# Layer 0's single-precision matmuls, the turned rows and the gram product side by side; the sum over d and the halves of x1 one to four groups sooner

## What is computed

```python
x0 = xk = stack([tbl_f[ids[:, f]] for f in range(39)], axis=1)   # (512, 39, 16)
for W in (f0, f1, f2):                 # (39*39, 128), (128*39, 128), (128*39, 128)
    z = einsum('bfd,bgd->bfgd', x0, xk).reshape(b, f * g, d)
    xk = einsum('bpd,pm->bmd', z, W); outs.append(xk)
z = sum(concatenate(outs, axis=1), axis=-1)                       # (512, 384)
h = relu(concatenate([z, dense_ctx], 1) @ W_top1 + b_top1)
y = relu(h @ W_top2 + b_top2) @ W_top3
```

## Time and profile before

| | us |
|---|---|
| median of 3 runs | 699.26 (698.6 to 702.59) |
| the profiled execution | 700.51 |
| its span | 698.7 |
| PE busy | 643.2 (92%) |
| VectorE, ScalarE, GpSimd busy | 538.7, 518.5, 429.9 (77, 74, 62%) |
| layer 1's matmuls (L789, L790, L793) of 512 columns, groups for ScalarE | 175.3, 152.2, 152.4 |
| the products on ScalarE (L640), x1536 | 440.7 |
| the steps on VectorE (L532), x960 | 266.0 |
| the half-sums on VectorE (L503), x128 | 223.6 |

### The profile page before, as it was taken

How to read it: one execution, slowest core, us unless ns; L and a number is a source line. 1 busy time by engine, 2 the same in 40 slices (tenths; PEclk the granted TensorE clock), 3 DMA queues, 4 the chain that set the end, 5 groups by cost and what they waited for, 6 DMA issues and landing times. The chain is left out here.

```text
span 698.7 us, 11739 instructions
## 1 busy us (share of the span) xinstructions
PE 643.2 (92%) x2567; PEld 472.3 (68%) x2567; DVE 538.7 (77%) x1216; ACT 518.5 (74%) x1842; POOL 429.9 (62%) x416
## 2 busy tenths in 40 slices
PE   0578999999999999999999999999999999999988
PEld 0246777676767677777777676767676777776663
DVE  1426788888887979797988888888979797999880
ACT  1226688788797878787887888787878787888862
POOL 6876568686767676767678686767676534101330
PEclk9877999999999999999999999999999999999999
DMA  7551332231304040313131221313040320301000
GB/s 206 117 118 30 88 74 45 45 72 37 80 10 106 9 107 3 85 31 77 39 77 40 56 61 39 77 23 93 9 108 4 96 63 0 109 0 44 29 1 0
DMA packets 58221, 40.28 MB, mean 58 GB/s; under 512 B 36626, under 2 KB 41056, under 8 KB 58203
## 3 DMA queue, kind: packets, MB, share of 16 engines
q1 hardware_dynamic: 52376, 38.73, 22.1%
q0 software_dynamic: 5120, 1.29, 2.4%
q10 hardware_dynamic: 706, 0.06, 0.1%
HBM read 38.13 MB, written 1.94 MB: 57 GB/s over the span
## 5 line engine op out<-in xcount | busy, mean ns | idle before, releaser
L640 ACT ACTIVATE parts<-psa,x0c 128x128 f32<-128x128 f32 x1536 | 440.7, 431 | 94.6 <-PE psa L793 88.2
L532 DVE SCALAR_TENSOR_TENSOR parts<-psd,x0c,parts 128x128 f32<-128x128 f32 x960 | 266.0, 342 | 80.9 <-PE psd L793 64.1
L503 DVE TENSOR_REDUCE cur<-parts 128x64 f32<-128x1536 f32 x128 | 223.6, 1747 | 23.7 <-ACT parts L640 18.8
L789 PE MATMUL psa<-w1h,x1h 128*128 128x512 f32 x384 | 175.3, 457 | 5.9 <-issue 5.9
L793 PE MATMUL psa<-w1h,x1l 128*128 128x512 f32 x384 | 152.4, 397 | 0.0
L790 PE MATMUL psa<-w1l,x1h 128*128 128x512 f32 x384 | 152.2, 396 | 0.0
L359 POOL TENSOR_TENSOR z0l<-pairs,z0h 117x512 fp32r<-117x512 f32 x56 | 72.7, 1298 | 122.6 <-ACT z0h L596 122.4
L343 POOL DMA_INDIRECT emb<-tables,idx x130 | 126.7, 975 | 23.3 <-issue 19.8
L352 POOL TENSOR_TENSOR pairs<-x0t,pairs 117x512 f32<-117x512 f32 (+1 forms) x105 | 135.1, 1296 | 7.3 <-DMA x0t<-x_rows 6.6
L789 PE MATMUL psd<-w1h,x1h 128*128 128x512 f32 (+1 forms) x256 | 115.2, 450 | 12.1 <-DVE parts L532 12.1
L793 PE MATMUL psd<-w1h,x1l 128*128 128x512 f32 (+1 forms) x256 | 97.8, 382 | 0.0
(11 more groups left out here) (83 smaller groups left out, 524.5 us busy)
## 6 DMA issues: line engine op xcount, KB each, us to landing
pairs<-x_rows SPq DMA_DIRECT2D x113, 156.0 KB
pairs<-x_rows SPq DMA_DIRECT2D x30, 234.0 KB
x0t<-x_rows SPq DMA_DIRECT2D x16, 234.0 KB
emb<-tables,idx POOLq DMA_INDIRECT x130
x_rows<-emb SPq DMA_DIRECT2D x13, 72.0 KB
wt_sb<-w_top SPq DMA_DIRECT2D x1, 768.0 KB, 5.9
parts<-w SPq DMA_DIRECT2D x1, 704.0 KB, 4.9
x_rows<-emb SPq DMA_DIRECT2D x13, 40.0 KB
```

What stands on the lines that cost most here:

```text
L503: return dve.tensor_reduce(cur1[:, t % 2, first:end], terms[:, first:end, :, :], AX.XY, ALU.add)
L532: op = dve.scalar_tensor_tensor(acc, y[:, M * j:M * j + M], x0c[:, t, GF * g + j:GF * g + j + 1], acc, ALU.mult, ALU.add)
L640: op = act.activation(lanes(dst, j), y[:, M * j:M * j + M], ACT.Copy, scale=x0c[:, t, GF * g + j:GF * g + j + 1])
L789: pe.matmul(y[:, 0:n], hi, w1h[:, c], start=True, stop=False)
```

## The change

On PE, step k = 0 moves from behind group 5 of tile 0, and k = 1 from behind group 7, to behind group 9; the turn moves from group 8 to group 9 as well, so that k = 0, k = 1, the turn and the gram product follow one another. Steps 2, 3 and 4 each move one slot on, k = 5 stays, and k = 6 goes last, behind group 9 of tile 1 and in front of its gram product. The turn itself becomes four ordinary matmuls of 39 rows by 128 columns with a 39 x 39 identity, in place of four transposes of 117 rows with a 117 x 117 one. On VectorE the sum over d moves from the third group of tile 2 to its first, the low part of tile 0 from the fourth to the second, of tile 1 from tile 3's first to tile 2's third. On ScalarE the high part of tile 0 moves from the fifth to the second group of tile 2, of tile 1 from tile 3's first to tile 2's fourth, of tile 2 from tile 3's third to its first. In block 0 only steps 5 and 6 change places, and so they do in the prologue.

```diff
-L0_AT = {(0, 5): 0, (0, 7): 1, (0, 9): 2, (1, 1): 3, (1, 3): 4, (1, 5): 6, (1, 8): 5}
-L0_AT_FIRST = {(1, 6): 0, (1, 8): 1, (2, 0): 2, (2, 2): 3, (2, 4): 4, (2, 6): 6, (2, 8): 5}
-TURN_AT, TURN_AT_FIRST = (0, 8), (1, 5)
+L0_AT = {(0, 9): [0, 1], (1, 1): [2], (1, 3): [3], (1, 5): [4], (1, 8): [5], (1, 9): [6]}
+L0_AT_FIRST = {(1, 6): [0], (1, 8): [1], (2, 0): [2], (2, 2): [3], (2, 4): [4], (2, 6): [5], (2, 8): [6]}
+TURN_AT, TURN_AT_FIRST = (0, 9), (1, 5)
...
-L0_END = 5
+L0_END = 6
...
-SUM_AT, SUM_AT_FIRST = (2, 2), (3, 0)
-HIGH_AT = {(2, 4): 0, (3, 0): 1, (3, 2): 2}
+SUM_AT, SUM_AT_FIRST = (2, 0), (3, 0)
+HIGH_AT = {(2, 1): 0, (2, 3): 1, (3, 0): 2}
...
-LOW_AT = {(2, 3): 0, (3, 0): 1, (3, 1): 2}
+LOW_AT = {(2, 1): 0, (2, 2): 1, (3, 1): 2}
...
-        ident_sb = sb("ident_sb", [128, ROWS])
+        ident_sb = sb("ident_sb", [128, F])
...
-                act.activation(x0c[:, t, 0:F], pst[:, ROWS * t:ROWS * t + F], ACT.Copy).then_inc(x0c_ready, 1)
+                act.activation(x0c[:, t, 0:F], pst[:, F * t:F * t + F], ACT.Copy).then_inc(x0c_ready, 1)
...
-                    op = pe.transpose(pst[:, ROWS * t:ROWS * t + ROWS], x0t[0:ROWS, 128 * t:128 * t + 128], ident_sb[0:ROWS, :])
+                    op = pe.matmul(pst[:, F * t:F * t + F], x0t[0:F, 128 * t:128 * t + 128], ident_sb[0:F, :], start=True, stop=True)
...
-                            if (t, g) in l0_at:
-                                layer0(b + 1, l0_at[t, g])
+                            for k in l0_at.get((t, g), []):
+                                layer0(b + 1, k)
...
-            for k in [*(k for k in range(L0T) if k != L0_END), L0_END]:
+            for k in range(L0T):
                 layer0(0, k)
```

More of the change, by code:

```diff
@@ L660, in block_of @@
                                 scalars(b + 1, SCALARS_AT[t, n])
-            act.dma_start(ident_sb[0:ROWS, :], ident).then_inc(const_in, 16)
+            act.dma_start(ident_sb[0:F, :], ident).then_inc(const_in, 16)
             act.dma_start(mask_sb[:, :], mask).then_inc(const_in, 16)
@@ L918 @@
         "sample_mask": samples.astype(np.float32),
-        "identity": np.eye(ROWS, dtype=np.float32),
+        "identity": np.eye(F, dtype=np.float32),
     }
```

## The result

The kernel became slower: 723.1 us median (720.42 to 724.4, 4 runs) against 700.6 (698.6 to 702.59; with one run more than the 699.26 of the table ahead), ratio 1.032 with a 95% interval of 1.030 to 1.034. That is 22.5 us; 14.3 were forecast, and the range ended at 718.5.

What follows compares the result with a forecast made beforehand. TensorE, 92% busy, was taken to bound the kernel, with 2.04 us of stalls a block from VectorE's lateness. Order 7.7 plus turn 6.6 gave 14.3; 700.5 became 714.8, less 1.25 for the median: 713.5 us, range 702 to 718.5.

Steps and rivals of the forecast that it cites:

- stalls: PE's waits in a block: 1.42 + 0.19 + 0.60 + 0.42 = 2.63 us against 2.04, so +0.59.
- Part 2, the turn: On PE, eight passes with weight loads of 0.107, the first hidden: 0.86 us against 0.42, +0.44 a turn.
- The upper bound, 0.9: Most that PE's turn should take in us, from load plus handover: +0.48 a turn.
- Rival A: The turn on PE is cheap, lower bound 0.27 us by streaming alone; chance 0.20.
- Part 1, tile 2: ScalarE stands 1.91 us at x1h(0) for VectorE's sum; PE stalls 1.42 us, new, before group 8.
- Tiles 3 and 0: PE's stalls for VectorE: 0.19 us at tile 3 group 6, 0.60 at its group 9, 0.42 in tile 0.
- The wait at k = 0: PE's 0.71 us stall for x1l at layer 0's first step, in tile 0, would be gone.
- Rival D: Worse: 3.1 us on PE without a group behind group 9 starves VectorE, 0.4 more a block, 719; chance 0.07.
- rival C: Gains and losses cancel: x1l's 0.71 wholly won, turn cheap, stall 1.0, total 697 to 702; chance 0.05.
- Part 3, side by side: Four fewer borders a block between rounded and single precision on PE: taken as 0, upper bound 1 us.
- Part 4, the loads: Row loads and x0t's load issue some 2.4 us later, without a wait; cost 0.
- Rival B: Not slower: the sum reaches ScalarE in tile 2 in time, psa never runs full, 688; chance 0.10.

Runs made afterwards that it cites:

- Run 8: The changed kernel with the identity's buffer as wide as before, so that all buffers behind it lie where the kernel before has them; 725.6 us.
- run 3: The changed kernel with its turn made of ordinary matmuls of all 117 rows by a 117 x 39 identity; 719.5 us, ratio 1.027.
- run 2: The kernel before with the new turn of four 39-row matmuls alone, at its old place; 710.4 us, ratio 1.012.
- run 1: The changed kernel with the four transposes of 117 rows back in the turn, all else as changed; 712.6 us, 1.019 of before.
- run 4: The kernel before with layer 0's new order and the turn behind group 9; transposes, sum and halves as before; 706.5 us, ratio 1.008.
- run 6: The kernel before with the sum one VectorE group sooner, and high parts and two low parts later; 683.0 us, ratio 0.975.
- run 9: The kernel before, transposes kept, with the identity's buffer moved last and a gap of 39 columns in its place; 699.7 us, ratio 0.998.
- run 10: The kernel before with later halves, and the identity's buffer moved last with a gap in its place; 678.9 us, ratio 0.971.

## Why the prediction was wrong

The direction, the main stall and its place were right; the turn was priced too low, and the size was short by 8 us and the range with it. The budget of a block, in us:

| term | forecast | measured |
|---|---|---|
| turn | +0.44 | +0.79 |
| stalls | +0.59 | +1.26 |
| pace of the rounded matmuls | 0 | -0.46 |
| sum | +1.03 | +1.59 |

The pace is what remains of the period after the other two; 108 matmuls by 4.0 ns are 0.43 of it. Run 8, the changed kernel at the old placement, has the two forecast terms without the pace: +0.79 and +0.87 give its 38.97 to 0.01. So the forecast of the turn was short by 0.35 and that of the stalls by 0.28. That the unforeseen pace and the longer stalls that it brings (-0.46 and +0.39) nearly cancel is luck. As an estimate, the turn's 0.35 over its 15 times is 5.3 us and the stalls' 0.28 over 14 blocks 3.9; pace and its stalls give back 1.0, and the median of the kernel before came out 1.4 higher than in the forecast. Together they lead from 713.5 to 723.1. The turn's part alone leads to 718.8, just past the range; the stalls' alone would have stayed inside, at 717.4.

**Part 2, the turn, is the step that failed**: forecast 0.86, measured 1.21. Its loads are 0.11 apart, eight of them, as worked out; "one load at a time is ahead of the matmuls, so the first hides" is false where the matmuls go from 117 rows to 39 and from 39 to 128: there the load starts only 0.07 before the drawn end of the matmul before it (0.12 and 0.20). The upper bound, 0.9, was thus no bound; it is what run 3, all of whose loads but the first are exposed, takes (0.89). The bracket asked what a pass costs and not what its neighbours lose, though a row of the kernel before had the answer. Rival A, a cheap turn, which the range takes in, fell altogether: no run shows the 0.27 of its lower bound. A turn of 39 rows takes 1.21 in the changed kernel and in run 2, and the loads stand 108 to 112 ns apart with 39 rows and 110 to 112 with 117 (run 3).

**Part 1, tile 2**: the new stall is 1.71 for 1.42. ScalarE was let go 4.84 after the tile's first products began (340.70 to 345.54); forecast were 4.64. Two handovers were taken too short: products to VectorE's steps 0.12 (340.70 + 1.16 to 341.98), not 0.04, and the sum to ScalarE 0.18 (344.68 + 0.68 to 345.54), not 0.08. PE's faster pace brought it to the bank 0.1 sooner: runs 1 and 8, at the old pace, have 1.61 here.

**Tiles 3 and 0**: 0.41, 0.63 and 0.56 for 0.19, 0.60 and 0.42. At the old pace (run 1) they are 0.32, 0.60 and 0.41. So two of the three were right. Group 6 of tile 3 was 0.13 short at the old pace, which no run explains, and the rest goes with PE's faster pace. The wait at k = 0 went as said. Rival D, the starving of VectorE by the long stretch behind group 9, did not come: the stalls of run 4 are 0.43 and 0.79 in tile 3, and 0.47 and 0.79 in tile 0, where 0.4 and 0.8 were expected. The gain of rival C, 0.71 at k = 0, came, but the turn wasn't cheap and the stall was 1.71 for its 1.0.

**Part 3, side by side worth nothing**: right (run 4). **Part 4, the loads**: right as far as seen. In the block shown, PE waits for ScalarE and VectorE alone, and for no transfer and not for GpSimd.

**What wasn't thought of**: that a smaller buffer moves every buffer behind it. "The smaller identity load is beside the prologue" priced the transfer alone.

**Rival B** put its deciding point right (x1h free within 0.5 us of ScalarE's arrival), but only in the direction of the change. Turned round it is run 6: ScalarE comes to x1h one group later, the sum is one group sooner, and 18 us are gained on the kernel before.

## What to carry to other kernels

Work such as a high part that one engine must make in order, in front of its steady work, belongs where its input is certainly there: asking one or two microseconds too soon stops the queue behind it for as long (0.75 and 1.03 us in the kernel before, 1.98 after), and the ring of three banks passed the 1.98 on to PE as a stall of 1.71. Small matmuls are to be priced by the weight loads and by the borders to their neighbours that the trace shows: eight passes of 39 columns cost 1.21 us where four transposes of 117 columns cost 0.42. And when matmuls are moved together, look at what they filled.

## What the hardware showed unexpectedly

- In these kernels a weight load isn't run ahead where the matmuls go from 117 rows to 39 and on to 128 (the changed kernel), from 128 to 39 and back (run 2), or from 128 to 16 and back (the MLP of the kernel before). It starts about 0.07 us before the drawn end of the matmul before it, after 0.76 us without a load behind a single-precision pass of 512 columns and 0.36 behind a rounded one. It cost 0.12 and 0.20 us at the two borders of the turn, and 0.19 between one such border and the next in the MLP. Between 78, 117 and 128 rows nothing of the kind shows (around k = 6 at most 0.24 without a load), so not every change of the number of rows does it; what happens between 39 and 78 rows, and why, no run shows.
- Rounded matmuls with the same instructions ran at 228.1 to 229.3 ns in five kernels with one placement of the buffers (the changed one and runs 2, 3, 9 and 10) and at 231.8 to 233.2 in nine with others (two more, with all behind the identity 256 and 512 bytes further on, at 230.0 and 230.2). The cause beyond the placement is open.
